# Kept blocks in pairs of row blocks, and a second DMA queue for the far rows of an adjacency product

## The reference

```python
A = adj + jnp.eye(8192)
deg = jnp.sum(A, axis=1)
d_isqrt = jax.lax.rsqrt(deg)
A_hat = A * d_isqrt[:, None] * d_isqrt[None, :]
h = jnp.matmul(jnp.matmul(A_hat, x), w)
x = layernorm(x + jax.nn.elu(h))      # no scale or shift, eps 1e-5
```

## Time and profile before

| | |
|---|---|
| median of three executions | 1069.43 us |
| the profiled execution | 1070.84 us, its span 1069.0 us |
| mean granted clock of PE | 0.965 |
| PE busy | 926.4 us (87%) |
| DVE, ACT, POOL busy | 784.5, 701.7, 199.1 us |
| DMA | 369.67 MB, mean 346 GB/s |
| adj loads on SP's queue | 337 of 1 MB |

### The profile page before, as it was taken

How to read it: one execution, slowest core, us unless ns; L and a number is a source line. 1 busy time by engine, 2 the same in 40 slices (tenths; PEclk the granted TensorE clock), 3 DMA queues, 4 the chain that set the end, 5 groups by cost and what they waited for, 6 DMA issues and landing times.

```text
span 1069.0 us, 36263 instructions
## 1 busy us (share of the span) xinstructions
PE 926.4 (87%) x16384; PEld 860.0 (80%) x16384; DVE 784.5 (73%) x661; ACT 701.7 (66%) x1689; POOL 199.1 (19%) x268
## 2 busy tenths in 40 slices
PE   0089299499498998989999999999999999999994
PEld 0087289498498997989999999879799998989994
DVE  0586587666767786868867899899888876867933
ACT  6888889888888898988988888830264627200202
POOL 0210120300403103041241344573111000000000
PEclk9999789799699999999999999999999999999997
DMA  9999999999999999999999999979798989899920
GB/s 379 397 394 406 394 396 404 393 401 398 395 395 389 396 379 398 381 394 387 397 391 400 390 382 364 345 248 372 248 287 288 312 266 317 252 311 310 365 89 21
DMA packets 171915, 369.67 MB, mean 346 GB/s; under 512 B 6256, under 2 KB 33520, under 8 KB 164080
## 3 DMA queue, kind: packets, MB, share of 16 engines
q1 hardware_dynamic: 154864, 358.96, 91.4%
q10 hardware_dynamic: 16896, 8.39, 2.7%
HBM read 363.13 MB, written 4.19 MB: 344 GB/s over the span
## 4 chain that ended last, share of the span: by engine, by line
PE 47%; issue 29%; DVE 7%; DMA 7%; POOL 7%; ACT 2%; SPq 1%; POOLq 0%; DVEq 0%; ACTq 0%
PE p_set L872 45%; DMA space<-in_adj 7%; POOL space L761 4%; DVE space L890 3%; DVE space L903 2%; PE p_set L850 2%; ACT space L778 1%; DVE hT L914 1%; SPq L723 1%; POOL xn L754 1%; POOL space L742 1%; POOL d L748 1%; ACT space L809 0%; DVE stats L943 0%; DVE space L937 0%
## 5 line engine op out<-in xcount | busy, mean ns | idle before, releaser
L872 PE MATMUL p_set<-space 32*128 32x256 f32 (+2 forms) x16256 | 908.8, 381 | 128.6 <-DVE space L903 60.3
L872 PEld LDWEIGHTS p_set<-space 32*128 32x128 f32 x16256 | 843.7, 187 | 189.6 <-issue 138.7
L890 DVE STREAM_TRANSPOSE space<-space 128x2048 f32<-128x2048 f32 x256 | 580.7, 2293 | 125.5 <-ACT space L778 94.0
L778 ACT ACTIVATE space<-space 128x512 f32<-128x512 f32 (+2 forms) x756 | 581.8, 770 | 99.0 <-DMA space<-in_adj 90.8
L914 DVE TENSOR_TENSOR hT<-p_set,hT 128x1024 f32<-128x1024 f32 (+1 forms) x107 | 105.0, 997 | 91.8 <-PE p_set L872 91.3
L778 ACT ACTIVATION_READ_ACCUMULATOR space<-space 128x1 f32 x756 | 141.0, 187 | 0.0
L801 ACT ACTIVATE space<-space 128x512 f32<-128x512 f32 x16 | 10.1, 630 | 191.5 <-DVE space L925 191.4
L761 POOL COPY space<-xn 32x512 f32<-32x512 f32 x192 | 123.3, 642 | 11.9
L748 POOL TENSOR_TENSOR d<-deg,half 128x4 f32<-128x4 f32 x16 | 16.3, 1019 | 538.2 <-DVE deg L896 538.1
L786 ACT ACTIVATE space<-xn 32x512 f32<-32x512 f32 x80 | 50.2, 627 | 40.6 <-POOL xn L754 34.9
L768 POOL TENSOR_TENSOR rstd<-var_eps,half 128x4 f32<-128x4 f32 x16 | 16.5, 1032 | 278.9 <-DVE var_eps L952 278.9
(11 more groups left out here) (15 smaller groups left out, 27.5 us busy)
## 6 DMA issues: line engine op xcount, KB each, us to landing
space<-in_adj SPq DMA_DIRECT2D x337, 1024.0 KB, 13.7
xn<-in_x SPq DMA_DIRECT2D x21, 256.0 KB, 12.3
space<-in_x ACTq DMA_DIRECT2D x16, 256.0 KB, 7.8
out_rows<-space ACTq DMA_DIRECT2D x16, 256.0 KB, 8.8
w_sb<-in_w SPq DMA_DIRECT2D x1, 64.0 KB, 1.8
```

Source lines behind the costliest of these rows:

```text
L778: ins = nc.scalar.activation(view[:, g], view[:, g], ACT.Copy, accum_out=to[:, g:g + 1])
L872: ins = nc.tensor.matmul(to, xs_chunk(h, j)[quadrant(q)], moving, start=first and s == b == 0, stop=last and s == b == 3)
L890: nc.vector.transpose(slots[slot], slots[slot]).then_inc(tile_turned, 1)
```

## The change

- `kept_units` now adds the kept blocks of a column in pairs of row bands (2i, 2i+1), nearest to the diagonal first, both or none; at an even column the diagonal block stands alone. `KEEP` is (12, 10, 8), `FEED` 12.
- Far loads go into ACT's order at rank 0 and are issued by ACT on its own DMA queue (`load_far`), after the same wait for the stage row, now on its own sums. SP's queue keeps the near loads, the tiles and x.
- Of the first copies of a band, ACT takes two of the four pieces of part 0.
- `out` may go without waiting for the z before it once all parts are given out.
- The last normalise is done by DVE, and the last store waits for that.

```diff
-KEEP = (12, 9, 7)
+KEEP = (12, 10, 8)
...
-FEED = 10
+FEED = 12
...
-FIRST_COPIES = [("dve", [(0, q) for q in range(Q)]), ("pool", [(s, q) for s in (1, 2, 3) for q in range(Q)])]
+FIRST_COPIES = [("dve", [(0, 0), (0, 1)]), ("act", [(0, 2), (0, 3)]), ("pool", [(s, q) for s in (1, 2, 3) for q in range(Q)])]
...
 def kept_units():
 
     alive, kept = [0] * BANDS, set()
-    for t, r in sorted(((t, r) for t in range(BANDS) for r in range(t + 1)), key=lambda v: (v[0], -v[1])):
-        if all(alive[m] < (KEEP[0] if m < KEEP[1] else KEEP[2]) for m in range(r, t + 1)):
-            kept.add((t, r))
-            for m in range(r, t + 1):
-                alive[m] += 1
+    for t in range(BANDS):
+        for r in range(t // 2 * 2, -2, -2):
+            rows = [u for u in (r, r + 1) if u <= t]
+            spans = [sum(u <= m for u in rows) for m in range(t + 1)]
+            if all(alive[m] + spans[m] <= (KEEP[0] if m < KEEP[1] else KEEP[2]) for m in range(r, t + 1)):
+                for u in rows:
+                    kept.add((t, u))
+                for m in range(r, t + 1):
+                    alive[m] += spans[m]
     return kept
...
-            return free_set() is not None and counts["residuals"] > 0 and counts["outs"] == counts["z"]
+            return free_set() is not None and counts["residuals"] > 0 and (counts["outs"] == counts["z"] or not parts_left())
...
+    def parts_left():
+        return sum(len(p[2]) for p in parts) < BANDS * BANDS
...
-            order["sp"].append(("load", k))
+            if load[0] == "far":
+                offer("act", 0, "load", k, 0.1)
+            else:
+                order["sp"].append(("load", k))
...
-            offer("act", 1, "normalise", arg, 1.7)
+            offer(*(("act", 1, "normalise", arg, 1.7) if arg < BANDS - 1 else ("dve", 1, "normalise", arg, 1.6)))
...
-                elif load[0] == "far" and row_before[arg] is not None:
-                    sp.wait_ge(act_summed, sum_nth[row_before[arg]])
...
+            def load_far(k):
+
+                if row_before[k] is not None:
+                    act.wait_ge(act_summed, sum_nth[row_before[k]])
+                act.dma_start(home_of(loads[k]), source(loads[k])).then_inc(arrival(k), 16)
...
-                act.wait_ge(normed, n + 1)
+                if n < BANDS - 1:
+                    act.wait_ge(normed, n + 1)
+                else:
+                    act.wait_ge(last_normed, 1)
...
+                elif kind == "normalise":
+                    n = arg
+                    dve.wait_ge(shift_ready, n + 1)
+                    for b in range(BLOCKS):
+                        ins = nc.vector.tensor_scalar(pos[:, n % RING, b], pos[:, n % RING, b], rstd[:, n % RING, b:b + 1],
+                                                      shift[:, n % RING, b:b + 1], ALU.mult, ALU.add)
+                    ins.then_inc(last_normed, 1)
```

More of the change, by code:

```diff
@@ L627, in gcn_resnorm @@
         normed = sem("normed")
+        last_normed = sem("last_normed")
         stored = [sem(f"stored{n}") for n in range(RING)]
@@ L823, in _ @@
                     row_sums(arg)
+                elif kind == "load":
+                    load_far(arg)
                 elif kind == "residuals":
```

## The result

The changed kernel takes 1113.45 us against 1069.06 for the kernel before, measured beside it: ratio 1.0416, 95% interval 1.0402 to 1.0429. That is 44.4 us slower where 2.3 us faster was forecast, and outside the range of 1055 to 1078. The profiled execution has a span of 1111.5 us and a mean granted clock of 0.951.

What follows compares the result with a forecast made beforehand. Transfers were taken to set the pace up to about 590 us, PE after it. From 1069.43 us, pairs +3.5, singles -2.0, copies -1.4, far loads 0 and tail -2.4 gave -2.3: 1067.1 us, range 1055 to 1078.

Steps and rivals of the forecast that it cites:

- Far loads on ACT: ACT's queue: 82 far issues fit into ACT's waits for data, and SP's lost waits were worth nothing; 0 us.
- Far rows push in ahead: Rival, DMA queues: next row's far loads delay this row's near loads, 2.7 us per megabyte; 1072.4 to 1077.8 us, chance 0.26.
- Two lanes move more: Rival, DMA transfers: small tile rows lose less beside long far rows on a second queue; 1055 us, chance 0.14.
- ACT blocks on its issues: Rival, ACT's queue: a full queue holds ACT's issues as it holds SP's; +34 us, about 1101, chance 0.10.
- Kept blocks in pairs: Before column 9: 130 instead of 131 blocks are ready, so PE starves 3.5 us earlier; cost 3.5 us.
- The other terms: Besides far loads at 0: pairs +3.5, fewer single parts -2.0, shared copies -1.4, tail -2.4; sum -2.3 us.
- Copies shared by DVE and ACT: First copies before column 9: ACT takes two of four, done near 589.8; 1.4 us gained, bound 1.3 lost.
- second-stage singles: Reloaded blocks from 899.69 us: two singles and a pair become two pairs; 0.9 us of the 2.0 gained by fewer singles.
- its holes: PE's idle gaps in the first stage, up to about 590 us, put at 66 us in all.
- From the last block to the end: The tail: output products follow each other and the last normalise moves to DVE; 2.4 us gained, bounds 0.7 to 2.8.
- DVE's last normalise: In the tail: DVE's four operations of 128x128, bounded at 0.6 to 2.8 us, taken as 1.0.

Runs made afterwards that it cites:

- e3: Changed kernel with every engine's order unchanged, but SP issues the far loads at their place among the tiles and ACT's load steps do nothing: 1086.67 us.
- e12: Changed kernel where SP, for loads 5 to 28 only, waits until load k-5 has landed before issuing load k: 1103.75 us.
- e14: Changed kernel with far loads issued by POOL on its own queue, SP and POOL both waiting for load k-5 to land: 1119.70 us.
- e6: Changed kernel with ACT issuing each far load right behind the sum that frees its stage row: 1127.79 us.
- e1: Changed kernel with far loads planned and issued on SP's queue again, behind SP's old wait, all other edits kept: 1065.31 us.
- e11: e3 with AHEAD 3 instead of 2, so the plan may go one row band further ahead: 1074.95 us.
- e16: e3 with SP sending each far load only after ACT has done all sums ahead of it in the changed kernel's ACT order: 1087.11 us.

## Why the prediction was wrong

**"Far loads on ACT ... I take 0"** is the step that failed, and in it one half sentence: SP's waits for ACT "were worth nothing while transfers never paused". The waits were read as idle time of an engine off the bound. They were the brake that kept one order: a kept block's load stood in SP's queue behind a far load that waited for its stage row, and so could not start before it. With the far loads on a queue of their own nothing holds the other loads back but free slots and the queue's own length, and in row 0 the kept loads went out at once. The waits did not disappear either: SP waits longer for slots. Price of this step: 26.8 us (after against e3), instead of 0, where its rival "Far rows push in ahead" had 5.3 to 10.7.

Taking the order of issue as free as long as transfers never pause would have needed a second look at the earlier trace rows: ACT is busy for 48.4 of 53 us in 428 to 481, so ACT consumes at nearly the rate at which loads land. Such a consumer has little with which to catch up: of the 12.4 us that e12 gives back in row 0, 9.7 are still there at the end. The text called this thin and yet costed it at nothing.

**"Far rows push in ahead"** had the mechanism (both queues share the engines, and a load that is not yet wanted passes one that is), and the direction wrong. It looked at far rows passing near loads; in after SP's loads passed the far rows (row 0's own kept blocks first), since SP was the engine that lost its wait. Its price of 2.7 us for each megabyte counted only the delay of the passed load. It left out that in-order ACT then stops, keeps stage rows full and starves the engines (e14). Whether the direction that it described exists as well is open: e6 is 14.3 us slower with early far issues, but no load was followed there.

The Trainium skill ("DMA: Bandwidth & Descriptors", "Issuing engines are not separate DMA queues") says that issuing from several engines at once saves only issue time. It was cited against *Two lanes move more*, and there the runs agree: 392 GB/s for one queue over 600 us, 378 for two, and 416 GB/s in 20 to 40 us of after, when both were busy, against 416 in 10 to 40 of before. It doesn't say that two queues are harmless. The section on queues of the same page, with its turns packet by packet, is the one that bears on the time, and the trace agrees: 810 packets of one queue against 804 of the other in 20 us, and far rows landed every 3.8 us with two busy queues, every 2.5 with one.

**"ACT blocks on its issues"** is empty: 0.335 us each at the median, 0.881 at the longest.

**"Kept blocks in pairs"** was costed by counts of blocks, and the counts were right: 130 blocks before column 9 put the hole before it at 4.03 us in e1 (3 to 4 forecast), with power 9 at 585.92 (within 2 us of 585 forecast). What the step left out is that `plan()` is rerun. The lane moves far loads into ACT's simulated time, this changes which part is taken when, and a leftover single block behind a pair of slots stops SP for 37 us. That is 21.4 us (e3 against e1), of which e11 names 11.7. No row of before could price it, but the order itself could have been written out for the changed plan, and its parts and slots read off.

**The other terms** come to -4.0 us where the lane is taken out (interval of the ratio: -5.6 to -2.2), against -2.3 forecast. That the sums lie close is partly luck, as the traces of before and e1 show (their spans differ by 5.1 us: 1069.0 and 1063.9). Column 9 starts 1.9 us later (593.16 against 591.25), for 2.1 forecast, but of other parts: the power 0.8 later, and then 7.24 us from power to first matmul instead of 6.16. *Copies shared by DVE and ACT*, costed at 1.4 gained, thus lost 1.1: ACT's two copies came behind the sums of the next tiles and ended at 592.9, not 589.8, and nearly the bound of 1.3 lost was the right end. The block that is missing before column 9 was multiplied afterwards, and the singles are gone: PE's work from column 9 to the last block is 455.2 us against 453.7, 1.5 more, for 1.6 forecast (3.5 less 5 x 0.37). What had hardly been costed are the small gaps in the same stretch: 6.9 us in before (among them the 2.08 and 0.65 of the earlier trace rows), 0.3 in e1. The forecast counted only what singles cost in length and half a microsecond of such a gap; that is the term which was too small, by about 6 us. (Its 0.9 us for the second-stage singles is also more than its own 14.4 less 13.9 gives, and its holes add up to 65, not 66; neither changes the result.) From the last block to the end it is 15.3 us in e1 and 17.2 in before, 1.9 gained for 2.4 forecast, with DVE's last normalise at 1.12 us for 1.0 taken.

**What stays open.** Of the queue's 26.8 us, 13.7 are there at row 0, shown by e12 to come from SP running ahead; 9.7 of them last to the end. The other 17.1 (e12 against e3) come later. Row 1's further delay is traced in e14, which is one row of one run. How the rest divides among later loads that are passed, full slots, the time that ACT can't make up, and anything else that two queues cost is not settled: no pacing by landings or sums came nearer to e3 than e12's 1103.75.

## What to carry to other kernels

A wait that stands in an in-order queue may be the only thing that orders what is behind it: before moving the work that waits, ask what else the wait held back, and what then comes first at the shared resource. If the consumer takes its inputs in a fixed order and is nearly as busy as the transfers, keep its loads in one queue in that order, as e1 does. When a change touches a planner's costs, compare the orders it gives out (leftover parts, which slot goes to whom) before costing anything by counts.

## What the runs showed of the hardware

- Two queues of 1 MB loads, both busy, shared the engines by packets and not by bytes: 810 and 804 packets in 20 to 40 us of after, but 5.87 MB on the queue of the 8 KB rows and 2.45 MB on the other. Far rows then land every 3.8 us instead of every 2.5. The sum of both was 416 GB/s there, as with one queue (416 in 10 to 40 us of before).
- An issue can stand without waiting for a semaphore: in after the eighth 1 MB load on SP's queue, behind seven others and x, took 26.9 us to issue, the first six 0.42 to 0.83 each.
- An issue on ACT's queue of a 1 MB load takes 0.335 us at the median with up to four in flight; on POOL's, 0.58 us as the mean of 82 (47.3 us).
- In e3 and e16, one queue with issue times shifted by whole sums of ACT, the time is the same within 0.4 us: with some five loads in flight (13.5 us from issue to landing in e3) a single late issue cost nothing.
